# Row and column groups on TensorE in the attention stage of a gated cross-attention and mixture-of-experts kernel

## Reference

```python
# attention: 16 query heads in 4 groups, 4 key/value heads, head size 16
q = rope(sum over groups of layernorm(x) @ Wq);  k = rope(ctx @ Wk);  v = ctx @ Wv
o = softmax(q @ k.T / 4) @ v, mean over the 4 heads, @ Wo
x = x + tanh(g_xattn) * o
# mixture: 8 experts, the best 2 for each row, expert width 1024
n = layernorm(x);  probs = softmax(n @ gate.T);  best two, weights normalised to 1
x = x + tanh(g_ffn) * sum over the two of weight * (silu(n @ Wg.T) * (n @ Wu.T)) @ Wd.T
```

## Time and profile before

| | |
|---|---|
| median of three runs | 466.45 us |
| the profiled execution | 466.44 us |
| its span, first to last instruction | 464.7 us |
| TensorE busy, mean granted clock | 424.1 us (91%), 0.946 |
| GpSimd, VectorE, ScalarE busy | 263.6, 214.3, 199.9 us |
| attention and routing | 0 to 131 us |
| expert stage | 131 to 464.7 us |

### The profile page before, as it was taken

How to read it: one execution, slowest core, us unless ns; L and a number is a source line. 1 busy time by engine, 2 the same in 40 slices (tenths; PEclk the granted TensorE clock), 3 DMA queues, 4 the chain that set the end, 5 groups by cost and what they waited for, 6 DMA issues and landing times.

```text
span 464.7 us, 10836 instructions
## 1 busy us (share of the span) xinstructions
PE 424.1 (91%) x2486; PEld 352.8 (76%) x2487; DVE 214.3 (46%) x571; ACT 199.9 (43%) x389; POOL 263.6 (57%) x264
## 2 busy tenths in 40 slices
PE   7899959784999999999999999999999999999950
PEld 6556646553578898888888888888888888889840
DVE  2465927476734443443434343444444443444330
ACT  2467733512175235625633733373336436523310
POOL 3118672578448544963982894279426954964321
PEclk9999976865799999999999999999999999999996
DMA  8950013642106412451462254115411641112210
GB/s 277 401 214 24 25 69 114 183 163 69 37 12 196 135 25 45 152 165 23 113 199 51 42 192 129 23 32 194 128 31 23 204 124 35 21 26 27 45 27 11
DMA packets 19563, 46.54 MB, mean 100 GB/s; under 512 B 2364, under 2 KB 13700, under 8 KB 16452
## 3 DMA queue, kind: packets, MB, share of 16 engines
q1 hardware_dynamic: 11632, 35.20, 22.2%
q0 software_dynamic: 6720, 9.64, 11.5%
q10 hardware_dynamic: 1188, 1.44, 0.9%
HBM read 37.54 MB, written 9.00 MB: 100 GB/s over the span
## 4 chain that ended last, share of the span: by engine, by line
PE 77%; POOL 9%; DVE 4%; DMA 3%; ACT 2%; issue 2%; POOLq 1%; SPq 0%; DVEq 0%; ACTq 0%
PE att L975 20%; PE sc L955 20%; PE misc L955 10%; PE qbank L955 10%; PE pT L965 6%; POOL dn L451 4%; PE sc L792 2%; DMA x<-in_x 2%; PE att L939 2%; PE misc L808 1%; PE sc L774 1%; POOL dn L391 1%; PE att L756 1%; PE att L831 1%; POOL hT L451 1%
## 5 line engine op out<-in xcount | busy, mean ns | idle before, releaser
L499 POOL DMA_INDIRECT out<-xT_all,index_out x34 | 54.5, 1604 | 109.1 <-DVE xT_all L1348 96.1
L975 PE MATMUL att<-dn,hT 128*128 x816 | 114.0, 289 | 1.5 <-DVE hT L1326 1.5
L975 PEld LDWEIGHTS att<-dn,hT 128*128 128x128 f32 x816 | 101.4, 189 | 2.1 <-issue 1.9
L955 PE MATMUL sc<-gu,xT 128*128 x408 | 101.9, 398 | 0.0
L955 PEld LDWEIGHTS sc<-gu,xT 128*128 128x128 f32 x408 | 74.1, 188 | 14.2
L955 PE MATMUL misc<-gu,xT 128*128 x204 | 80.0, 392 | 1.6 <-ACT xT L678 0.8
L955 PE MATMUL qbank<-gu,xT 128*128 x204 | 79.9, 392 | 0.0
L385 POOL TENSOR_TENSOR gu<-wraw,gu 128x2048 f32 x14 | 64.5, 4628 | 9.1 <-ACT gu L595 7.1
L1322 DVE TENSOR_TENSOR xT_all<-xT_all,sc 128x512 f32<-128x512 f32 x34 | 23.4, 689 | 87.2 <-ACT xT_all L685 87.2
L685 ACT ACTIVATE xT_all<-misc 128x512 f32<-128x512 f32 x34 | 20.3, 598 | 74.9 <-PE qbank L955 71.7
L1322 DVE TENSOR_TENSOR xT_all<-xT_all,qbank 128x512 f32<-128x512 f32 x34 | 23.4, 687 | 57.8 <-ACT xT_all L685 57.8
(11 more groups left out here) (157 smaller groups left out, 522.0 us busy)
## 6 DMA issues: line engine op xcount, KB each, us to landing
wraw<-in_gu SPq DMA_DIRECT2D x16, 1024.0 KB, 5.4
wraw<-in_dn SPq DMA_DIRECT2D x8, 1024.0 KB, 5.2
x<-in_x SPq DMA_DIRECT2D x8, 266.0 KB, 11.2
xT_all<-in_xT SPq DMA_DIRECT2D x4, 512.0 KB, 11.3
out<-x SPq DMA_DIRECT2D x8, 256.0 KB, 2.3
rows_scratch<-x SPq DMA_DIRECT2D x3, 532.0 KB, 3.8
xT_all<-rows_scratch,index_in POOLq DMA_INDIRECT x37, 2.9
out<-xT_all,index_out POOLq DMA_INDIRECT x34, 3.9
```

Of the source, the lines that this page charges most:

```text
L499: nc.gpsimd.indirect_dma_start(out=out_d, out_offset=bass.IndirectOffsetOnAxis(ap=index, axis=0), in_=y[:, r, :], in_offset=None, compute_ ...
L955: mm = nc.tensor.matmul(bank[2 * hf + n][:, :], xT[:, par, xp, k, :], gu_part(where, wp, k * 2 * I + col, HALF), start=(k == 0 and xp == 0 ...
L975: mm = nc.tensor.matmul(bank[6][:, 0:D], hT[:, hf, hp, j * P:(j + 1) * P], dn_part(where, wp, (hf * JH + j) * D, D), start=(hf == 0 and j ...
```

## The change

Everything is in the attention stage. Scores are two products of 64 rows of contraction and 240 columns for each tile j, one for each half of the partitions, into two banks. The four heads' products with the values, and four products with a table `sums` for the denominators, put each head into its own 32 partitions (a "quad") of `o_ps` and `sums_ps`; the gate's two chunks go ahead into quads 0 and 1. The heads come out transposed as they are needed, so `transpose_o` and `copy_oT` go away, and `normalise_o` writes `oT` itself. `attend` also adds x by a product with the identity, `second_moments` reads PSUM, and ScalarE copies the rows to SBUF (`copy_rows`). GpSimd splits the third piece at t = 4, and set g is inverted one iteration later. `ranks` of the last set goes ahead of the last inversions. Tables and tiles (`wo`, `woT`, `gc_quad`, `v`) are widened to fit, `kbd` is halved, `probsT` moves into another buffer.

```diff
-        o_ps = misc[:, 0:TB * OW].rearrange("p (j h d) -> p j h d", j=TB, h=KVH)
-        oT_ps = misc[0:KO, OT_AT:OT_AT + S]
+        o_ps, sums_ps = misc[:, 0:S], misc[:, S:2 * S]
...
-            nc.gpsimd.memset(v[:, :, :, :], 1.0).then_inc(fills, 1)
+            nc.gpsimd.memset(v[:, :, :, :], 0.0).then_inc(fills, 1)
...
+            nc.gpsimd.memset(gc_quad[:, :, :], 0.0).then_inc(fills, 1)
+            nc.gpsimd.memset(probsT[:, :, :], 1.0).then_inc(fills, 1)
...
-                if t in (1, 2):
-                    split_low_first(t)
-                if t == 2:
+                if t in (1, 4):
+                    split_low_first(1 if t == 1 else 2)
+                if t == 4:
                     pool.wait_ge(w_lo_first, 3 * (PIECE // CHUNK))
                     pool.sem_inc(w_lo, 3)
...
-            def copy_oT(b):
-                act.wait_ge(oT_psum, b + 1)
-                if b >= 1:
-                    act.wait_ge(att_psum, b)
-                nc.scalar.activation(oT[:, :], oT_ps, ACT.Copy).then_inc(oT_ready, 1)
+            def copy_rows(b):
+                act.wait_ge(att_psum, b + 1)
+                act.wait_ge(moments2, TB * (b + 1))
+                nc.scalar.activation(x[:, TB * b:TB * b + TB, 0:D], att[:, :, 0:D], ACT.Copy).then_inc(x2_ready, 1)
...
             for t in range(B + 1):
                 if t < B:
                     copy_pT(t, 0)
-                if t >= 1:
-                    copy_oT(t - 1)
...
+                if t >= 1:
+                    copy_rows(t - 1)
                 if t < 3:
                     split_high(0, t)
...
+            def scores(b):
...
+                    pe.wait_ge(exp_done, TB * b)
+                for j in range(TB):
+                    for q in range(PAIR):
+                        rows = slice(HR * PAIR * q, HR * PAIR * (q + 1))
+                        mm = nc.tensor.matmul(sc[:, q, PAIR * A * j:PAIR * A * (j + 1)], qrot[rows, b % 2, P * j:P * (j + 1)],
+                                              kbd[rows, b, :, :].rearrange("p h a -> p (h a)"), start=True, stop=True)
+                mm.then_inc(s_psum, 1)
...
+            def mix_values(b):
+
                 if b >= 1:
                     pe.wait_ge(oT_ready, b)
+                quad = lambda ap, n: ap[QUAD * n:QUAD * (n + 1), :]
+                for k in range(KC):
+                    nc.tensor.matmul(quad(o_ps, k), gc_quad[:, k, :], xT_all[:, k, S * b:S * (b + 1)],
+                                     start=True, stop=False)
+                pe.wait_ge(pT_copied, TB * (b + 1))
                 for hh in range(KVH):
+                    nc.tensor.matmul(quad(o_ps, hh), v[:, b, hh, :], probsT[:, hh, :], start=(hh >= KC), stop=True)
+                for hh in range(KVH):
+                    mm = nc.tensor.matmul(quad(sums_ps, hh), c("sums"), probsT[:, hh, :], start=True, stop=True)
+                mm.then_inc(o_psum, 1)
...
-                mm = nc.tensor.matmul(att[:, j, 0:D + E], oT[:, P * j:P * (j + 1)], wo[:, :], start=True, stop=True)
+                pe.wait_ge(x_in[b], 16)
+                nc.tensor.matmul(att[:, j, 0:D + E], oT[:, P * j:P * (j + 1)], wo[:, :], start=True, stop=False)
+                mm = nc.tensor.matmul(att[:, j, 0:D], ident, x[:, TB * b + j, 0:D], start=False, stop=True)
...
-                if t < B and t - 3 in ENDS:
+                if t < B and t - 4 in ENDS:
                     pe.wait_ge(x2_ready, t - 1)
-                    group = SETS[ENDS[t - 3]]
+                    group = SETS[ENDS[t - 4]]
                     for b in group:
                         invert(b, group[0], group[-1])
-                for j in range(TB):
-                    if t >= 1:
+                if t >= 1:
+                    for j in range(TB):
                         attend(t - 1, j)
-                    if t < B:
-                        mix_values(t, j)
+                if t < B:
+                    mix_values(t)
...
             def normalise_o(b):
                 dve.wait_ge(o_psum, b + 1)
+                link(V.reciprocal(rden[:, :], sums_ps))
                 if b >= 1:
-                    dve.wait_ge(oT_psum, b)
-                link(V.reciprocal(rden[:, :, :], o_ps[:, :, :, HD]))
-                V.tensor_tensor(on[:, :, :, :], o_ps[:, :, :, 0:HD],
-                                rden[:, :, :].rearrange("p j (h o) -> p j h o", o=1).broadcast_to([P, TB, KVH, HD]),
-                                ALU.mult).then_inc(on_ready, 1)
+                    dve.wait_ge(att_psum, b)
+                V.tensor_tensor(oT[:, :], o_ps, rden[:, :], ALU.mult).then_inc(oT_ready, 1)
...
-            def add_residual(b):
-                rows = x[:, TB * b:TB * b + TB, 0:D]
-                V.tensor_tensor(rows, att[:, :, 0:D], rows, ALU.add).then_inc(x2_ready, 1)
```

More of the change, by code:

```diff
@@ L69 @@
 NS = len(SETS)
-OT_AT = TB * OW
+PAIR = KVH // 2
 RANK_AT = KVH * A
-KO = KVH * HD + E
+QUAD = P // KVH
+assert HD + E <= QUAD and A < P
 INV_AT = D + E
@@ L85, in _const_columns @@
     at = 0
-    for name, n in (("ident", P), ("kcos", A), ("ksin", A), ("rope", S), ("before", P), ("prio", E),
+    for name, n in (("ident", P), ("kcos", A), ("ksin", A), ("rope", S), ("sums", QUAD), ("before", P), ("prio", E),
                     ("base", E), ("limits", E * NT), ("earlier", E * E), ("blocks", NCOL),
@@ L114, in build_program @@
         wka, wkb, wv, gw, gates = (kvw[:, a:b] for a, b in ((0, 256), (256, 512), (512, 640), (640, 656), (656, 658)))
-        wo = sb("wo", [KO, D + E])
-        woT = sb("woT", [P, KC, KVH * HD])
-        gc = sb("gc", [P, KC, E])
+        wo = sb("wo", [P, D + E])
+        woT = sb("woT", [P, KC, P])
+        gc_quad = sb("gc_quad", [P, KC, QUAD])
+        gc = gc_quad[:, :, HD:HD + E]
         wqc = sb("wqc", [P, KC, P])
@@ L142, in build_program @@
         wq = raw_wq[:, :, 0, :]
[L143 to L144 removed]
+        oT = sb("oT", [P, S])
         tg = sb("tg", [P, 2])
@@ L783, in project_q @@
                 mm.then_inc(q_psum, 1)
[L785 to L789, removed]
+            def scores(b):
+                pe.wait_ge(qrot_ready, b + 1)
+                pe.wait_ge(kbd_ready, 1 if b < KEYS[0][1] else 2 if b < KEYS[1][1] else 3)
                 if b >= 1:
-                    pe.wait_ge(exp_done, TB * (b - 1) + j + 1)
-                nc.tensor.matmul(sc[:, j, 0:KVH * A], qrot[:, b % 2, P * j:P * (j + 1)],
-                                 kbd[:, b, :, :].rearrange("p h a -> p (h a)"), start=True, stop=True).then_inc(s_psum, 1)
+                    pe.wait_ge(exp_done, TB * b)
[5 more added lines that the diff above has]
+                mm.then_inc(s_psum, 1)
             def transpose_probs(b, j):
@@ L882, in _ @@
             for k in range(KC):
-                mm = nc.tensor.matmul(misc[0:KVH * HD, WOG_AT:WOG_AT + E], woT[:, k, :], gc[:, k, :],
+                mm = nc.tensor.matmul(misc[:, WOG_AT:WOG_AT + E], woT[:, k, :], gc[:, k, :],
                                       start=(k == 0), stop=(k == KC - 1))
             mm.then_inc(wog_psum, 1)
-            scores(0, 0)
-            scores(0, 1)
+            scores(0)
             project_keys(1, att[:, 0, :], att[:, 1, :])
@@ L893, in _ @@
             for t in range(B + 1):
-                if t + 1 < B:
-                    scores(t + 1, 0)
                 if t < B:
@@ L928, in _ @@
                 invert(b, late, B - 1)
-            ranks(NS - 1)
             invert(B - 2, late, B - 1)
@@ L1120, in choose @@
                  .then_inc(chosen_ready, 1)
-            def add_residual(b):
-                rows = x[:, TB * b:TB * b + TB, 0:D]
-                V.tensor_tensor(rows, att[:, :, 0:D], rows, ALU.add).then_inc(x2_ready, 1)
             def second_moments(b):
-                dve.wait_ge(x2_ready, b + 1)
-                moments(b, stats2, mv2, moments2)
+                dve.wait_ge(att_psum, b + 1)
+                for j in range(TB):
+                    V.bn_stats(stats2[:, TB * b + j, :], att[:, j, 0:D]).then_inc(dve_step, 1)
+                    n_step[0] += 1
+                for j in range(TB):
+                    dve.wait_ge(dve_step, n_step[0] - TB + 1 + j)
+                    V.bn_aggr(mv2[:, TB * b + j, :], stats2[:, TB * b + j, :]).then_inc(moments2, 1)
             def logit_gap(g):
@@ L1252, in _ @@
                     best_two(t - 1)
-                    if t < B and t - 3 in ENDS:
-                        add_places(ENDS[t - 3])
+                    if t < B and t - 4 in ENDS:
+                        add_places(ENDS[t - 4])
                     if t == B:
                         logit_gap(NS - 1)
-                    add_residual(t - 1)
+                    if t < B:
+                        second_moments(t - 1)
                 if t < B:
@@ L1263, in _ @@
                         logit_gap(ENDS[t - 1])
-                if t >= 1:
-                    second_moments(t - 1)
+            second_moments(B - 1)
             ranks_of_picks(NS - 1)
@@ L1398, in shape_constants @@
```

(1 more changed line is left out.)

95 lines of the change are left out of this document (44 added, 51 removed).

## The result

The kernel after takes 460.15 us, the median of 8 runs (458.26 to 463.53), where the kernel before takes 466.61 us beside it (8 runs, 464.63 to 468.44): a ratio of 0.9877, 95% interval 0.9837 to 0.9916. It is faster, but by 6.5 us, a third of the 20.4 us forecast, and its time lies 0.15 us above the range. The profiled execution took 459.30 us, its span is 457.5 us. The eight runs differ by the clock that TensorE was granted: four with a mean of 0.954 took 458.26 to 459.61 us, the profiled one among them, and four with 0.943 to 0.947 took 460.70 to 463.53.

A forecast was written before the change was run, and what follows sets the result against it. TensorE bounds the expert stage, whose start hangs on GpSimd's line in attention. Marks of set 2 come 20.5 us earlier, the 17.1 and 15.8 us behind them stay: 466.4 - 20.5 = 446.0 us, range 442 to 460.

The forecast's parts named there:

- The 15.8 us from the last inversion to the loop: Before the expert loop: filling matmuls, gather and tables keep their code, so 15.8 us stay.
- GpSimd's 17.1 us behind the marks of set 2: GpSimd's line from the marks of set 2 to the last inversion, 17.1 us, expected to stay.
- 5.2 forecast: TensorE's attention iteration: products of one group run fully beside each other, 5.2 us, against 6.5 before.
- rivals C and D: TensorE groups: C, little or no overlap, 452 to 465 us, 0.16; D, serial plus emptying at shape changes, 472, 0.08.
- The marks of set 0 stand ahead of the third split: Sign on GpSimd: marks of set 0 precede the third split, start at about 53 and end near 60 us.
- I take 0.42: Reciprocal over 256 columns in `normalise_o` on VectorE: costs what the query rotation does, 0.42 us.
- rival B: VectorE becomes the bound: reciprocal costs 1.47 us, marks of set 2 at 82.3, time 451 us; chance 0.13.
- upper bound of 1.47 us: Reciprocal in `normalise_o` at worst: each further column costs 5.1 ns, 1.47 us in all.
- 77.6: Start of the marks of set 2 on GpSimd, forecast at 77.6 us instead of 98.09.
- gaps of GpSimd before `second_norm`: Sign of VectorE as the bound: GpSimd has gaps before `second_norm` while VectorE is full.
- Nearly all of it is the order: Attention stage: with TensorE left at 6.5 us an iteration, the order alone reaches 78.7, a us later only.
- 1.00 from 12 to 80 us: Sign on TensorE: clock at 1.00 without a gap over 3 us from 12 to about 80 us.

The follow-up runs named there:

- short_reciprocal: Kernel after with the reciprocal taken over 8 of 256 columns and reused for all; 477.64 us, ratio 1.0231, with 37 blocks run instead of 34.
- short_late_split: short_reciprocal with the third split moved behind the expert stage's tables; 474.21 us, ratio 1.0163, with 37 blocks run instead of 34.
- split_behind_tables: Kernel after with the third split moved behind the expert stage's tables; 456.82 us, ratio 0.9780.
- order_only: Kernel before with only the order changed: third split at t = 4, every set inverted one iteration later; 457.47 us, ratio 0.9804.
- residual_order: order_only with x added by TensorE, moments from PSUM and rows copied by ScalarE; 460.75 us, ratio 0.9859.

## Why the prediction failed

**Right.** The expert stage did not change. The 15.8 us from the last inversion to the loop are 15.56, GpSimd's 17.1 us behind the marks of set 2 are 17.9. Groups of one mode run side by side: the ten products take 1.4 us against 4.8 one after another, the iteration 5.3 us against 5.2 forecast. So rivals C and D do not hold; changes of shape show no step of 0.3 us (from the last score to the transposes at 41.30 there is none). The marks of set 0 stand ahead of the third split. The Trainium skill, TensorEngine Tiling (Array Packing), Key Properties, has both rules, tiles of a mode in parallel and a drain at a change of mode; the trace agrees with the first and bounds the second at below a few tenths of a us here.

**The step that failed: "I take 0.42" for the reciprocal.** It is 1.73 us. The prediction had rival B for this, priced at 451 us with an upper bound of 1.47 us, worked out from two short reciprocals, of 1 and 8 columns. Both rows are mostly fixed cost, so a slope between them was good for a direction, not for a bound: 1.73 us less the 0.16 of one column, by 255, is 6.2 ns for each column, not 5.1. The prediction also allowed that most of what the eight columns cost above the one came from the source in PSUM. The product of 256 columns has a source in PSUM too and takes 0.42 us, so the source alone does not make 1.73; no run takes the wide reciprocal from SBUF, so its share is open. The Trainium skill, VectorE: DVE Perf Modes, First, the fixed hardware budget, says that this engine's reciprocal is an iterative divide with a repeat count of 8; it gives no time for it, but speaks against pricing it like a product, and the traces agree (1.73 and 0.42 us at 256 columns). Taken out, it returns 10.1 of the 11.7 us by which the marks missed 77.6.

**The term that was not in the sum: GpSimd's split blocks VectorE.** The third split was only moved, and costed as GpSimd's time. At its new place it runs beside `choose` of set 1 and stretches four small operations from 0.19 to about 1.1 us, while VectorE is the bound and TensorE waits. This is 3.4 us (short_reciprocal to short_late_split, and 89.31 to 86.00 for split_behind_tables). The two together, 13.5 us, put the marks at 75.81, 1.8 us ahead of the forecast: the miss is accounted for. Rival B was the right mechanism, and its sign is in the trace (gaps of GpSimd before `second_norm`, 1.54 and 2.43 us, while VectorE is full), but its price was too low. Not only by the reciprocal: with 1.31 us instead of 1.05 in its five iterations its own sum gives marks at 83.6, where split_behind_tables, without the stretched `choose`, has 86.00. No run explains these 2.4 us. The time itself follows: 446.0 + 11.7 for the marks, 0.8 for the line behind them (17.9 for 17.1), -0.2 for the tail and 1.0 in the expert stage give 459.3, the profiled execution.

**"Nearly all of it is the order" was wrong as worked out.** The order alone gives marks at 92.91, not 78.7. That sum held a clock of 1.00, and iterations of 6.5 us read from one place. What the groups gain on TensorE (the iteration falls to 5.3 us) is real and was needed to come near 78: with the reciprocal short and the split away the marks are at 75.81, while with only the scores in groups and the split away they are at 84.15 to 87.09. In the kernel after, the 1.31 us by which each reciprocal exceeds the forecast hide it. So the order is worth 9.9 us alone (and 4.6 us with the groups in, 464.75 to 460.15), and the groups, as built, nothing that these runs can tell on top of it.

**The clock.** It was to be 1.00 from 12 to 80 us, with no gap of TensorE over 3 us. It is 0.86 from 48 to 60 and 0.80 from 60 to 72; a wait of 1.85 us at 49.85 and the one of 5.48 us stand ahead of pieces at 1.2 GHz. In short_late_split, where these waits are 0.91 and 0.22 us, it is 1.00 to 72 us.

## What to carry to other kernels

Before a reduction to few columns is replaced by a wide one to please another engine, price the wide form of the very operation: a reciprocal of 256 columns costs four products, and a slope from two short ones is no bound. When a block of GpSimd work is moved, look at what VectorE does in that stretch, not only at GpSimd's own line; put it beside operations that did not stretch here (beside the split in order_only the query rotation, which reads PSUM, took its usual 0.41 us, and a reduction 0.20). And once the engine that waits is served earlier, ask which line is next: here the marks of set 2 came at 98.09 behind GpSimd's line, at 92.91 behind TensorE's and at 89.31 behind VectorE's, so each gain was good only up to the next one.

## What the runs showed of the hardware

*VectorE and GpSimd exclude each other.* The Trainium skill, SBUF — State Buffer, Who interferes with whom, says that the two share a pair of ports under an exclusive lock, taken by VectorE's operations with two SBUF inputs against GpSimd's reads, or by its copies, conversions and scalar operations in a two-port mode, and that `tensor_reduce` never contends. The traces agree: `TENSOR_TENSOR` 0.97 to 1.19 us beside the split instead of 0.19, `TENSOR_REDUCE` 0.18. It goes both ways: of the marks of set 0 in the kernel after, one takes 1.84 us instead of 0.79, in the stretch in which VectorE's `mark_slots` (from 53.49, 1.34 us) has two inputs in SBUF, and all eight 7.31 instead of 6.26. In order_only the conversions do it too:

```profile
74.03 0.20 DVE L1148 TENSOR_REDUCE slot_i<-route 128x8 int32<-128x64 f32 x1
74.27 1.07 DVE L1150 TENSOR_SCALAR slot_i<-slot_i 128x8 int32<-128x8 int32 x1
75.36 1.19 DVE L1151 CAST slot_f<-slot_i 128x16 f32<-128x16 int32 x1
```

Here each stands for about one chunk of 1.24 us. The 4.46 us of the tables' conversion are more than that rule says for single instructions: it stood through all that was left of four separate chunks. Why it did not come in between two of them, as others did, is open.

*The clock can fall on an engine that is hardly idle.* order_only shows 0.86 from 36 to 48 us with TensorE busy 11.37 us and its longest wait there 0.60 us at 36.96; the clock falls in `project_q` at 39.66. residual_order shows 1.00 with 11.37 and a little more work of another kind, behind the same three waits of 1.03, 0.92 and 0.60 us, all 1.14 us later than in order_only:

```profile
36.00:48.00 12.00, 11.37 (x59) 7.20 (x58) 6.09 (x19) 9.05 (x18) 7.77 (x8) 1.00 0.07 23
```

What decides between the two is not settled here. The shortfall of the clock in order_only from 36 to 84 us is 6.8 us of work.
